# Gathered rows in eight buffers, and two slot computations moved ahead of one transpose: one change to a two-layer MoE kernel

## The chip, the cores and the metric

The kernel runs on 1 core of one Trainium2 chip. The metric is device microseconds of one execution; 163.64 us is the median of 3 runs (163.5 to 164.37). Lower is better. In this text PE is TensorE (PEld its weight loads), DVE is VectorE, ACT is ScalarE, POOL is GpSimd and SP is SyncE.

## The reference

Input is 1,024 tokens of 128 features. Two layers follow each other, each a conditioning step and a mixture of 8 experts, with a residual add:

```python
x = x + L0_ffn(L0_cond(x))     # layer one: every token goes to its 2 best of 8 experts (relu, 512 wide)
x = x + L1_ffn(L1_cond(x))     # layer two: every expert picks its best tokens

# L1_ffn, the part that the second edit touches
n = b * l; k = n * 2 // 8                       # 1024 tokens, 256 for each expert
S = sigmoid(xt @ Wg).T
G, I = top_k(S, k)                              # the 256 best tokens of each expert
ex = xt[I]                                      # gathered rows
hid = gelu(einsum('ekh,ehf->ekf', ex, W1) + b1)
out = (einsum('ekf,efh->ekh', hid, W2) + b2) * G[..., None]
new_x = zeros_like(xt).at[I.reshape(-1)].add(out.reshape(-1, h))
```

## The kernel before, in words

Each engine has one instruction stream, written out by hand, in program order; engines wait for each other on semaphores. Loads and stores go out on SP's queue (some on ACT's); everything indexed goes out on POOL's queue as an indirect DMA, one instruction for 128 rows.

**Layer one.** The 2,048 (token, expert) pairs are sorted by expert into 16 blocks of 128 rows. POOL gathers blocks 1 to 15 into the ring `xs` (`gather(b)`, L454), `RING` buffers deep: gather `b` waits until PE has transposed block `b - RING` out of the same buffer. PE transposes a block (`turn_x(b)`, L592), ACT copies it out of PSUM, and PE does the two matrix products of a block with an expert (`up`, L617; `down0`, L627), 23 such pairs in all, DVE adding the results up (`keep`, L1233). Behind the gathers on POOL stand the 16 scatters of the results (`scatter(b)`, L459); scatter `b` waits for pair `b + 8` to be kept.

**Layer two.** Experts 0 to 6 are computed on gathered rows, 256 each, as units `HEAD` to `UNITS - 1` (`HEAD` is 4: units 0 to 3 are expert 7 done on all tokens). For each of these experts `e` the steps are:

- `place(e)` (DVE, L1369): a one-hot matrix of the rows' places, 128x1024 bf16, double buffered, so `place(e)` waits for `find_slots(e - 2)`.
- `find_slots(e)` (PE, L770): 8 small matmuls with it give the row numbers. For `e` of 2 and more it waits for `index(e - 1)`.
- `index(e)` (DVE, L1116): copies the row numbers to SBUF as integers.
- `gather1(e)` (POOL, L476): two indirect DMAs of 128 rows. Below, gather (e, h) is half h of expert e. All 14 stand in order on POOL's queue; behind them stand the scatters `add(e)` (L483) of the results of experts 0 to 4 into scratch planes in HBM, 10 in all, each waiting for its result in `y1`.
- `turn_xg(e)` (PE, L781): two transposes of the gathered rows; `take_xg(e)` (ACT, L1023) copies them out.
- `up1(n, h)` (PE, L709): four matmuls, `gelu(n, h)` (ACT, L1032), and `down_both(n)` (PE, L818): 16 matmuls.
- `score` (DVE, L1398) writes the result `y1`.

DVE's order is `place(0)`, `place(1)`, `index(0)`, then `index(e - 1)`, `place(e)` in turn for e from 2 to 6, then `index(6)`, then the scores, with the whole-width add `take_dense` (L1427) behind the scores of expert 0. In the end SP loads each plane back in two halves once its scatters have landed, and DVE adds them to the sum (`take_part`, L1416); the results of experts 5 and 6 are spread by PE (L829) instead. ACT's order at the start of the gathered units is `take_xg(0)`, `gelu(4, 0)`, `take_xg(1)`, `gelu(4, 1)`, `gelu(5, 0)`, `take_xg(2)`.

Of the kernel before, what the change touches and what calls it, by code (L numbers as in the profile page):

```python
# [32 lines left out]
H = 256  # L33
K = 2
LORA_SCALE = 32.0 / R
RING = 4
WB_RING = 4
NB = K * T // P
NPAIR = NB + E - 1
# [3 lines left out]
SPARSE = 7  # L43
# [69 lines left out]
def adaln_moe(nc, xT, x, first, second, rows, w1, w2, cond_w, gate_w, v1, c1, v2, consts, out):  # L113
    with ExitStack() as ctx:
        def sb(name, shape, dt=F32):
            return ctx.enter_context(nc.sbuf_tensor(name, shape, dt))

        def sem(name):
            return ctx.enter_context(nc.semaphore(name))
# [90 lines left out]

        xs = sb("xs", [P, RING, C])
        w1_now = sb("w1_now", [P, WB_RING, FW])
# [96 lines left out]

        gathered = [sem(f"gathered_{q}") for q in range(RING)]  # L310
        h0_ready = sem("h0_ready")
# [126 lines left out]
        def _(pool):  # L438
# [7 lines left out]
            def rows_at(idx, i):  # L446
                return bass.IndirectOffsetOnAxis(ap=idx[:, i:i + 1].bitcast(U32), axis=0)
# [3 lines left out]
            def gather(b):  # L451
                if b >= RING:
                    pool.wait_ge(x_turned, b - RING + 1)
                pool.indirect_dma_start(out=xs[:, b % RING], out_offset=None, in_=rows0,  # L454
                                        in_offset=rows_at(gidx, b)).then_inc(gathered[b % RING], 16)

# [45 lines left out]
        def _(pe):  # L502
# [196 lines left out]
            def up1(n, h, parts=(0, 1)):  # L699
                dense, e, q = unit[n]  # L700
                rows_in = dT[:, CAP * q:CAP * q + CAP] if dense else xgT[:, e % 2]
                if not dense:
                    pe.wait_ge(xgT_ready, e + 1)
                u = 2 * n + h
                if u >= 4:
                    pe.wait_ge(h1T_ready, 2 * (u - 4) + 2)
                for f in parts:
                    fc = 2 * h + f
                    mm = pe.matmul(bank[UP_BANKS[u % 4]][:, CAP * f:CAP * f + CAP], v1_sb[:, e, P * fc:P * fc + P],  # L709
                                   rows_in, start=True, stop=True)  # L710
                    if f == 1:
                        mm.then_inc(h1_ready, 1)
# [49 lines left out]
            def find_slots(e):  # L762
                pe.wait_ge(onehot1, e + 1)
                if e < 2:
                    for hlfv_part in hlfv_ready:
                        pe.wait_ge(hlfv_part, e + 1)
                if e >= 2:
                    pe.wait_ge(idx1_ready, 1 if e == 2 else e)
                for c in range(NC):
                    mm = pe.matmul(bank[SLOT_BANKS[e]][:, 0:2 * NH], one1[:, e % 2, :, c],  # L770
                                   hlfv[:, c, e].rearrange("p v h -> p (v h)"), start=(c == 0), stop=(c == NC - 1))
                mm.then_inc(slots1, 1)

            def turn_xg(e):
                pe.wait_ge(gathered1[e], 16 * NH)
                if e == 0:
                    pe.wait_ge(idx1_ready, 2)
                if e >= 1:
                    pe.wait_ge(xgT_ready, e)
                for h in range(NH):  # L780
                    mm = pe.transpose(bank[0][:, P * h:P * h + P], xg[:, e * NH + h, 0:C], ident)  # L781
                mm.then_inc(xg_turned, 1)
# [21 lines left out]
            def down_both(n):  # L804
                e = unit[n][1]
                pe.wait_ge(h1T_ready, 4 * n + 2)
                if n == HEAD:
                    pe.wait_ge(yd_kept, HEAD)
                if n == HEAD + 1:
                    pe.wait_ge(idx1_ready, SPARSE)  # L810
                for g in range(2):
                    if g == 1:
                        pe.wait_ge(h1T_ready, 4 * n + 4)
                    for h in range(NH):
                        if g == 0 and NH * (n - HEAD) + h >= 3:
                            pe.wait_ge(y1_kept, NH * (n - HEAD) + h - 2)
                        for f in (2 * g, 2 * g + 1):
                            mm = pe.matmul(bank[y_bank(n, h)][:, C * h:C * h + C], h1T[:, n % 2, f, P * h:P * h + P],  # L818
                                           v2_sb[:, e, f], start=(f == 0), stop=(f == NF - 1))
                        if g == 1:  # L820
                            mm.then_inc(y1_sent, 1)
# [46 lines left out]
            turn_xg(0)  # L868
            find_slots(3)
            up1(HEAD, 0)  # L870
            turn_xg(1)
            find_slots(4)
            up1(HEAD, 1)
            for n in range(HEAD + 1, UNITS):
                e = n - HEAD
                if 1 < e and e + 1 < SPARSE:
                    turn_xg(e + 1)
                up1(n, 0)
                if n == HEAD + 1:
                    find_slots(SPARSE - 2)  # L880
                    turn_xg(2)
                if n == UNITS - 1:
                    up1(n, 1)
                down_both(n - 1)
                if n == HEAD + 1:
                    find_slots(SPARSE - 1)
                if n < UNITS - 1:
                    up1(n, 1)
# [5 lines left out]
        def _(act):  # L894
# [140 lines left out]
            def take_yd(n):  # L1035
                _, e, q = unit[n]
                act.wait_ge(y1_sent, NH * n + NH)
                act.activation(yd[:, e - SPARSE, NH * q:NH * q + NH], bank[6 + n % 2][:, 0:NH * C], ACT.Copy).then_inc(yd_kept, 1)
# [473 lines left out]
```

## Time and profile before

| | |
|---|---|
| median of 3 runs | 163.64 us (163.5 to 164.37) |
| span of the profiled execution, first to last instruction | 150.0 us |
| profiled execution's own time | the page gives its span alone; the median lies 13.64 us above the span |
| PE busy | 138.6 us, 92% |
| PE weight loads busy | 122.1 us, 81% |
| DVE busy | 94.5 us, 63% |
| ACT busy | 84.9 us, 57% |
| POOL busy | 61.4 us, 41% |
| granted TensorE clock, mean | 0.991 of full speed |

The busy times are averages over stages with different limits. What matters for a change is which wait ends last at the place that it touches; for that the trace is read instruction by instruction, as start, length, engine, line, and what ended the idle time before it. The chain of the page gives 68% of the span to PE, 14% to DVE, 5% to DMA and 3% to POOL.

### The profile page before, as it was taken

The numbers are of one execution on the slowest core, as the hardware profiler recorded it, in microseconds if no ns is written. First come the engines' busy times: TensorE is split into PE (matmuls) and PEld (weight loads), VectorE is DVE, ScalarE is ACT, GpSimd is POOL, SyncE is SP. The second block draws the span as 40 slices with busy tenths as digits, with TensorE's granted clock in tenths as the row PEclk, the third lists the DMA queues.
The fourth block names the chain that finished last, engine by engine and source line by source line (L and its number), as shares of the span: only waits on it lengthen the run. The fifth ranks groups of instructions, "written<-read, shape, count | busy, mean of one in ns | idle before, by whom it ended". The sixth has DMA issues, their size and how long they took to land.

```text
span 150.0 us, 3681 instructions
## 1 busy us (share of the span) xinstructions
PE 138.6 (92%) x1139; PEld 122.1 (81%) x1139; DVE 94.5 (63%) x323; ACT 84.9 (57%) x259; POOL 61.4 (41%) x65
## 2 busy tenths in 40 slices
PE   7999887999999999999999997979998999999970
PEld 3765777999999999964789975748988999999960
DVE  5467947555556565452699777767242597748891
ACT  0688826777777666620377769985326255557400
POOL 5000376544477555560500000003677778777000
PEclk9999999999999999999999999999999999999996
DMA  4999614999999991113602940030022222457714
GB/s 142 357 403 315 216 37 89 312 367 393 394 396 342 300 331 37 38 36 88 211 0 116 400 190 0 0 153 2 19 56 50 56 50 59 152 174 236 254 47 140
DMA packets 12965, 26.10 MB, mean 174 GB/s; under 512 B 2082, under 2 KB 5538, under 8 KB 12562
## 3 DMA queue, kind: packets, MB, share of 16 engines
q1 hardware_dynamic: 10336, 21.54, 40.9%
q0 software_dynamic: 1760, 3.67, 8.1%
q10 hardware_dynamic: 850, 0.66, 1.3%
q8 instruction: 10, 0.16, 0.4%
q14 instruction: 9, 0.07, 0.2%
HBM read 19.92 MB, written 5.93 MB: 172 GB/s over the span
## 4 chain that ended last, share of the span: by engine, by line
PE 68%; DVE 14%; DMA 5%; issue 4%; ACT 3%; POOL 3%; DVEq 0%; ACTq 0%
PE bank L617 13%; PE bank L627 13%; PE bank L709 10%; PE bank L818 7%; PE bank L676 3%; PE bank L581 3%; DVE c_tok L1416 2%; POOL xg L476 2%; PE bank L685 2%; DMA got<-picked 2%; PE bank L508 2%; PE bank L770 2%; DMA xg<-rows,idx 2%; DMA picked<-y,sidx 1%; PE bank L543 1%
## 5 line engine op out<-in xcount | busy, mean ns | idle before, releaser
L952 ACT ACTIVATE hT<-bank,w_now 128x128 f32<-128x128 f32 x88 | 25.1, 368 | 11.5 <-PE bank L617 11.5
L1032 ACT ACTIVATE h1T<-bank,c_sb 128x256 f32<-128x256 f32 x44 | 18.3, 471 | 13.7 <-PE bank L709 13.7
L454 POOL DMA_INDIRECT xs<-rows,gidx x15 | 15.1, 1006 | 24.1 <-DVE gidx L1186 14.6
L627 PE MATMUL bank<-w_sb,hT 128*128 (+1 forms) x184 | 24.4, 276 | 0.3 <-ACT hT L952 0.3
L617 PE MATMUL bank<-xg,w_now 128*128 (+1 forms) x176 | 23.4, 276 | 0.8 <-ACT xg L936 0.8
L627 PEld LDWEIGHTS bank<-w_sb,hT 128*128 128x128 f32 x184 | 22.4, 192 | 0.5 <-ACT hT L952 0.5
L617 PEld LDWEIGHTS bank<-xg,w_now 128*128 128x128 f32 x176 | 21.4, 192 | 1.1 <-issue 1.0
L459 POOL DMA_INDIRECT picked<-y,sidx x16 | 15.7, 979 | 10.0 <-DVE y L1233 8.5
L476 POOL DMA_INDIRECT xg<-rows,idx x14 | 14.8, 1054 | 5.0 <-issue 3.7
L1233 DVE SCALAR_TENSOR_TENSOR y<-bank,pairm,y 128x128 f32 (+1 forms) x23 | 8.1, 351 | 10.2 <-PE bank L627 10.0
L709 PE MATMUL bank<-xgT,v_sb 128*128 128x256 f32 x56 | 14.2, 384 | 0.0
L488 POOL TENSOR_TENSOR hlfv<-hlf1h,cst 128x16 bf16<-128x16 bf16 (+1 forms) x2 | 1.3, 692 | 30.6 <-DVE hlf1h L1365 30.6
L1225 DVE SCALAR_TENSOR_TENSOR y<-b_sb,pairm,y (+1 forms) x23 | 8.1, 351 | 8.5 <-issue 7.8
L818 PEld LDWEIGHTS bank<-v_sb,h1T 128*128 128x128 f32 x96 | 11.6, 192 | 0.3
L483 POOL DMA_INDIRECT plane<-x_sb,idx x10 | 10.5, 1049 | 3.0 <-issue 2.1
L818 PE MATMUL bank<-v_sb,h1T 128*128 128x128 f32 x96 | 11.7, 275 | 0.0
L508 PE MATMUL bank<-ones 128*128 128x512 bf16 x41 | 10.6, 416 | 1.1 <-DVE ones L1118 1.1
L1207 DVE COPY w_now<-w_sb 128x516 f32 (+1 forms) x22 | 9.8, 446 | 2.1 <-issue 1.9
L709 PEld LDWEIGHTS bank<-xgT,v_sb 128*128 128x128 f32 x56 | 9.8, 192 | 1.0
L800 PE MATMUL bank<-v_sb,h1T 128*128 128x128 f32 x80 | 10.1, 278 | 0.0
L800 PEld LDWEIGHTS bank<-v_sb,h1T 128*128 128x128 f32 x80 | 9.5, 192 | 0.2
L709 PE MATMUL bank<-w_eff,v_sb 128*128 128x256 f32 x32 | 9.1, 393 | 0.0
(214 smaller groups left out, 246.9 us busy)
## 6 DMA issues: line engine op xcount, KB each, us to landing
v_sb<-in_v SPq DMA_DIRECT2D x16, 256.0 KB
cw_sb<-in_cond_w SPq DMA_DIRECT2D x8, 386.5 KB
plane<-y SPq DMA_DIRECT2D x5, 512.0 KB, 5.1
w_sb<-plane SPq DMA_DIRECT2D x10, 256.0 KB, 3.1
w_sb<-in_w SPq DMA_DIRECT2D x2, 1024.0 KB, 7.6
w_sb<-in_w SPq DMA_DIRECT2D x1, 1290.0 KB, 7.9
w_sb<-in_w SPq DMA_DIRECT2D x1, 774.0 KB, 5.8
rows<-row SPq DMA_DIRECT2D x1, 544.0 KB, 3.3
```

Of the source, the lines that this page charges most:

```text
L454: pool.indirect_dma_start(out=xs[:, b % RING], out_offset=None, in_=rows0, in_offset=rows_at(gidx, b)).then_inc(gathered[b % RING], 16)
L459: pool.indirect_dma_start(out=picked, out_offset=rows_at(sidx, b), in_=y0[:, b], in_offset=None).then_inc(scattered, 16)
L476: pool.indirect_dma_start(out=xg[:, i], out_offset=None, in_=rows1, in_offset=rows_at(idx1, i)).then_inc(gathered1[e], 16)
L483: pool.indirect_dma_start(out=plane[e], out_offset=rows_at(idx1, i), in_=y1[:, e % Y1_RING, h], in_offset=None).then_inc(added[e], 16)
L508: pe.matmul(out_bank[:], ones[:], ones[:].unsqueeze(1).to_broadcast([P, 4, P]), start=True, stop=True)
L617: mm = pe.matmul(bank[2 + j % 2][:, P * f:P * f + P], w1_of[:, P * f:P * f + P], xsT[:, bass.ds((j - e) * P, P)], start=True, stop=True)
L627: mm = pe.matmul(bank[6 + j % 2][:, 0:C], hT[:, j % 2, P * f:P * f + P], w2_sb[:, bass.ds(e * (NF * C) + f * C, C)], start=(f == 0), stop= ...
L709: mm = pe.matmul(bank[UP_BANKS[u % 4]][:, CAP * f:CAP * f + CAP], v1_sb[:, e, P * fc:P * fc + P], rows_in, start=True, stop=True)
L800: mm = pe.matmul(bank[y_bank(n, h)][:, C * h:C * h + C], h1T[:, n % 2, f, P * h:P * h + P], v2_sb[:, e, f], start=(f == 0), stop=(f == NF ...
L818: mm = pe.matmul(bank[y_bank(n, h)][:, C * h:C * h + C], h1T[:, n % 2, f, P * h:P * h + P], v2_sb[:, e, f], start=(f == 0), stop=(f == NF ...
L952: ins = act.activation(hT[:, j % 2, P * f:P * f + P], bank[2 + j % 2][:, P * f:P * f + P], ACT.Relu, bias=w1_of[:, F + f:F + f + 1])
L1032: act.activation(h1T[:, n % 2, fc], bank[UP_BANKS[(2 * n + h) % 4]][:, CAP * f:CAP * f + CAP], ACT.Gelu, bias=c1_sb[:, e * NF + fc:e * NF ...
```

## The change

The ring of gathered rows of layer one gets eight buffers in place of four. In layer two, PE's stream at the start of the gathered units is put in another order: `turn_xg(1)` comes behind `find_slots(4)` and the second half of the first unit's up-product, and `find_slots(5)` (written `SPARSE - 2`) comes ahead of the second unit's up-product.

```diff
-RING = 4
+RING = 8
@@ -868,16 +868,16 @@
             turn_xg(0)
             find_slots(3)
             up1(HEAD, 0)
-            turn_xg(1)
             find_slots(4)
             up1(HEAD, 1)
+            turn_xg(1)
+            find_slots(SPARSE - 2)
             for n in range(HEAD + 1, UNITS):
                 e = n - HEAD
                 if 1 < e and e + 1 < SPARSE:
                     turn_xg(e + 1)
                 up1(n, 0)
                 if n == HEAD + 1:
-                    find_slots(SPARSE - 2)
                     turn_xg(2)
```

On PE, from the transpose of expert 0's rows to the first down-product of the gathered experts, the rows stood like this (L781 is `turn_xg`, L770 `find_slots`, L709 `up1`, L818 `down_both`):

```order
L781 MATMUL bank<-ident_sb,xg 128x128 x2
L770 MATMUL bank<-hlfv,slot1h 128x4 x8
L709 MATMUL bank<-xgT,v_sb 128x256 x2
L781 MATMUL bank<-ident_sb,xg 128x128 x2
L770 MATMUL bank<-hlfv,slot1h 128x4 x8
L709 MATMUL bank<-xgT,v_sb 128x256 x4
L770 MATMUL bank<-hlfv,slot1h 128x4 x8
L781 MATMUL bank<-ident_sb,xg 128x128 x2
L818 MATMUL bank<-v_sb,h1T 128x128 x8
```

Now they stand like this:

```order
L781 MATMUL bank<-ident_sb,xg 128x128 x2
L770 MATMUL bank<-hlfv,slot1h 128x4 x8
L709 MATMUL bank<-xgT,v_sb 128x256 x2
L770 MATMUL bank<-hlfv,slot1h 128x4 x8
L709 MATMUL bank<-xgT,v_sb 128x256 x2
L781 MATMUL bank<-ident_sb,xg 128x128 x2
L770 MATMUL bank<-hlfv,slot1h 128x4 x8
L709 MATMUL bank<-xgT,v_sb 128x256 x2
L781 MATMUL bank<-ident_sb,xg 128x128 x2
L818 MATMUL bank<-v_sb,h1T 128x128 x8
```

The second L781, expert 1's transpose, moved behind one L770 and one L709; the third L770 moved ahead of the last L709. (The order counts a float32 product as one row; the trace shows it as two matmuls.) The streams of DVE, ACT, POOL and SP keep their order.

On POOL, layer one's gathers and the first scatter, with the semaphores that they wait for, before:

```order
L454 DMA xs<-rows,gidx 128x128 [waits rows0_written,idx_ready]
L454 DMA xs<-rows,gidx 128x128 x2
L454 DMA xs<-rows,gidx 128x128 [waits x_turned] x12
L459 DMA picked<-y,sidx 2048x128 [waits y_kept,sidx_ready]
```

And now:

```order
L454 DMA xs<-rows,gidx 128x128 [waits rows0_written,idx_ready]
L454 DMA xs<-rows,gidx 128x128 x6
L454 DMA xs<-rows,gidx 128x128 [waits x_turned] x8
L459 DMA picked<-y,sidx 2048x128 [waits y_kept,sidx_ready]
```

Four of the fifteen gathers lost their wait for a transpose, and the other eight wait for one that lies four blocks further back.

## Rows read from the trace of the kernel before

**Rows 1.** Page, head of the profile.

```profile
span 150.0 us, 3681 instructions
```

**Rows 2.** Timeline, PE: start us, length us, line, operation, [idle before <- releaser].

```profile
111.40 1.13 PE L709 MATMUL bank<-xgT,v_sb 128*128 128x256 f32 x4
112.99 0.44 PE L781 MATMUL bank<-ident_sb,xg 128*128 128x128 f32 x2 [0.46 <-DMA xg<-rows,idx]
113.27 0.60 PE L770 MATMUL bank<-hlfv,slot1h 128*128 128x4 bf16 x8
113.73 1.97 PE L709 MATMUL bank<-xgT,v_sb 128*128 128x256 f32 x8
115.54 0.60 PE L770 MATMUL bank<-hlfv,slot1h 128*128 128x4 bf16 x8
116.00 0.42 PE L781 MATMUL bank<-ident_sb,xg 128*128 128x128 f32 x2
```

**Rows 3.** Timeline, POOL, gathers of layer two: (1,1), (2,0), (2,1), (3,0), (5,1).

```profile
110.41 0.94 POOL L476 DMA_INDIRECT xg<-rows,idx  x1 [0.30 <-issue]
111.66 1.33 POOL L476 DMA_INDIRECT xg<-rows,idx  x1 [0.30 <-DVE idx L1116]
113.29 0.94 POOL L476 DMA_INDIRECT xg<-rows,idx  x1 [0.30 <-issue]
114.53 0.95 POOL L476 DMA_INDIRECT xg<-rows,idx  x1 [0.30 <-issue]
...
120.79 1.51 POOL L476 DMA_INDIRECT xg<-rows,idx  x1 [0.30 <-issue]
```

**Rows 4.** Timeline, DVE, same stretch: places 4, 5, 6, index 4, the dense add.

```profile
111.49 0.68 DVE L1369 TENSOR_TENSOR slot1h<-xT_sb,loc 128x1024 bf16<-128x1024 bf16 x1
113.91 0.16 DVE L1116 TENSOR_REDUCE idx<-bank 128x2 int32<-128x4 f32 x1 [1.74 <-PE bank L770]
113.99 0.68 DVE L1369 TENSOR_TENSOR slot1h<-xT_sb,loc 128x1024 bf16<-128x1024 bf16 x1
...
116.26 0.68 DVE L1369 TENSOR_TENSOR slot1h<-xT_sb,loc 128x1024 bf16<-128x1024 bf16 x1
...
120.27 1.22 DVE L1427 TENSOR_TENSOR w_sb<-w_sb,c2b_sb 128x1024 f32<-128x1024 f32 x1
```

**Rows 5.** Timeline, ACT, gelu(4, 0) and take_xg(1).

```profile
112.63 0.84 ACT L1032 ACTIVATE h1T<-bank,c_sb 128x256 f32<-128x256 f32 x2 [1.28 <-PE bank L709]
113.47 0.38 ACT L1023 ACTIVATE xgT<-bank 128x256 f32<-128x256 f32 x1
```

**Rows 6.** Timeline: POOL's first and last add, DVE's scores of expert 4.

```profile
125.16 1.05 POOL L483 DMA_INDIRECT plane<-x_sb,idx  x1 [0.30 <-issue]
...
137.42 0.96 POOL L483 DMA_INDIRECT plane<-x_sb,idx  x1 [0.30 <-issue]
133.38 0.80 DVE L1398 SCALAR_TENSOR_TENSOR x_sb<-bank,xg,gb 128x128 f32<-128x128 f32 x2 [2.38 <-PE bank L818]
```

**Rows 7.** Timeline and DMA issues, the tail: last plane load, DVE's last six adds.

```profile
140.03 0.43 SPq L378 DMA_DIRECT2D w_sb<-plane  x1
w_sb<-plane SPq DMA_DIRECT2D x1, 256.0 KB, 4.9
141.66 3.98 DVE L1416 TENSOR_TENSOR c_tok<-c_tok,w_sb 128x512 f32<-128x512 f32 x6
```

**Rows 8.** Layer one: landing of its gathers (min/median/max), timeline of PE and POOL.

```profile
DMA to landing us min/median/max: 2.4/5.6/6.8
34.79 0.27 PE L592 MATMUL bank<-ident_sb,xs 128*128 128x128 f32 x1
27.75 0.94 POOL L454 DMA_INDIRECT xs<-rows,gidx  x1 [0.66 <-PE bank L592]
41.11 0.94 POOL L454 DMA_INDIRECT xs<-rows,gidx  x1 [0.95 <-PE bank L592]
49.05 0.97 POOL L459 DMA_INDIRECT picked<-y,sidx  x1 [0.45 <-DVE y L1233]
```

## The prediction

> **What bounds the kernel now.** I read the page first, then the waits, then the timelines of the two stretches that the diff touches, then the tail. The span is 150.0 us and the median of the runs 163.64 us, so 13.64 us lie around the span [rows 1]; I make the sum in span time and carry that difference over unchanged, since nothing of it is touched.
>
> In layer one PE runs back to back. In layer two there is one hole in front of it, at `turn_xg(1)`: the transpose starts at 112.99 after 0.46 us in which PE waited for gather (1,1) to land [rows 2]. The part that the busy shares hide is POOL: it is 41% busy, but from gather (1,1) at 110.41 [rows 3] to the end of the last add at 138.38 [rows 6] it never waits for anybody. Each gather takes 0.94 us and the next follows 0.30 us later, so 1.25 us apart [rows 3], and the adds go on at once from 125.16 to 137.42 [rows 6]. The last add (4,1) could have started at 134.18, when its score was written, 3.2 us before it did [rows 6]. So the adds hang on POOL's own pace, not on PE.
>
> In the tail the two paths meet. The last plane half is issued at 140.03 and lands 4.9 us later, at 144.93; DVE's six adds run from 141.66 to 145.64, one each 0.66 us, so the sixth, which needs that half, starts near 144.96 [rows 7]. PE's path (over the last scores and DVE) and POOL's path (over adds and loads) reach the end within 0.1 us of each other. **A gain on PE alone is therefore worth nothing at the end, and a loss on either is paid in full.**
>
> **Eight buffers in layer one: 0.** Gather 8 started at 27.75, when a transpose had freed its buffer, and its block was transposed at 34.79, 7.04 us later; the gathers landed 5.6 us (median) and at worst 6.8 us after their start [rows 8]. That is 0.24 us of margin in the worst case, and no transpose waited. With eight buffers POOL goes at 1.25 us a gather: the last starts near 27.75 + 7 x 1.25 = 36.5 in place of 41.11, 4.6 us earlier [rows 3, 8]. The first scatters can follow earlier, but by scatter 5 (49.05) they wait for DVE's sums, as before [rows 8]. What could be hidden here has been hidden already; what hides it is PE's work, and if that cover were gone the wait would be at most 0.24 us per block from the worst landing alone. Cost: the gathers share the DMA engines with the weight loads earlier, with unchanged bytes. A bound from below and above is the spread of landing itself, 5.6 against 6.8 us, 1.2 us on a load; no PE instruction of this stage waits for a load, so I take 0.
>
> **The new order in layer two, on PE.** `up1(4, 0)` starts at 111.40; eight such matmuls take 1.81 us (113.73 to 115.54), so four 0.90: PE is free at 112.30 [rows 2]. `find_slots(4)` no longer stands behind the transpose. Its one-hot is ready (place 4 ends at 112.17 [rows 4]), so it starts at 112.30 in place of 113.27, 0.97 us earlier; it takes 0.46 us to the next product [rows 2]. The moved steps issue no DMA; POOL asks for the row numbers of expert 4 only at 114.53 + 2 x 1.25 = 117.03 [rows 3], and had them since 114.07 [rows 4], so having them earlier starts no gather earlier. `up1(4, 1)` goes to 113.66, and `turn_xg(1)` then finds its rows landed since 112.99: the wait of 0.46 us is gone. `find_slots(5)` follows 0.28 us later, at 113.94 (its one-hot: below). `up1(5, 0)` needs ACT's copy of the transpose. Before, that copy began 0.48 us behind the transpose and took 0.38 [rows 2, 5]; with some 0.05 for the signal PE can go on at 113.66 + 0.91 = 114.57, 0.17 us after `find_slots(5)`. Its four matmuls end at 115.47, and PE stands before `turn_xg(2)`, 0.53 us earlier than its start at 116.00 before [rows 2].
>
> **What it waits for there.** Gather (1,1) ended at 111.35 on POOL and its rows were used at 112.99, 1.64 us later. Gather (2,1) ends at 114.23 [rows 3], so its rows are there at 115.87 and no earlier. Of the 0.53 us won only 0.13 are left, if POOL stays as it was. The stall is not removed, it is moved to the next expert.
>
> **What moves on POOL.** It does not stay as it was. Gather (2,0) started at 111.66 inside place 4 (111.49 to 112.17) and took 1.33 us in place of 0.94; gather (5,1) at 120.79 inside the dense add (120.27 to 121.49) took 1.51 [rows 3, 4]. Both were longer by what was left of the DVE operation less some 0.12 us (0.51 left, 0.39 longer; 0.70 left, 0.57 longer). Gather (2,1), which ran when place 5 began at 113.99, took 0.94, and (3,0), 0.14 us before its end, 0.95. So a gather that starts in such an operation stands until it is over.
>
> The Trainium skill ("SBUF — State Buffer", section "Who interferes with whom") says that a DVE instruction with two SBUF inputs holds off a GpSimd one that reads SBUF for its whole length, and the first comer wins; the trace agrees for these two. The same section infers that this kind, tensor_tensor, leaves descriptor generation alone; by that the two hits below would not come, and the sum would be 163.5. The rows decide.
>
> With `find_slots(4)` at 112.30, index 4 comes 0.64 us later as before (113.27 to 113.91), at 112.94, and place 5 runs from 113.02 to 113.70 [rows 2, 4]. Gather (2,1) starts at 113.29, inside it: 0.41 left, 0.29 longer. `find_slots(5)` at 113.94 gives index 5 at 114.58 and place 6 from 114.66 to 115.34; gather (3,0), now at 114.82, is inside that one: 0.52 left, 0.40 longer. Before, place 6 ran at 116.26 and held up nobody.
>
> So the rows of (2,1) are there at 115.87 + 0.29 = 116.16, and `turn_xg(2)` starts 0.16 us **later** than before. From there PE has no other wait, so all of it, and DVE's scores behind it, is 0.16 us late. POOL is late by 0.69 us, until the dense add: it runs at 120.43 to 121.65, gather (5,1) starts at 121.48 inside it, 0.17 left, 0.05 longer in place of 0.57. POOL is then 0.69 - 0.52 = 0.17 us late. This is a catch: whoever starts in the dense add ends with it, so POOL's delay becomes DVE's own. Both paths reach the tail 0.16 to 0.17 us late. **Sum:** 150.0 + 0.17 + 13.64 = 163.81 us, 0.1% more.
>
> **The rivals.**
> - *No new hits* (the DVE places miss the gathers' starts by some tenths, or do not hold them off). `turn_xg(2)` at 115.87, 0.13 us earlier; the dense add 0.13 earlier, which holds (5,1) to the same end: 163.64 - 0.13 = 163.51. For: place 5 is hit with 0.27 us to spare on one side, but the second hit hangs on the first (without it gather (3,0) starts at 114.53, ahead of place 6). 27%.
> - *PE's gain arrives whole*: the 0.46 us of waiting [rows 2] go and the tail follows, 163.18. Against it: the last half lands when DVE needs it, and gather (2,1) paces. 8%.
> - *Slower, by POOL*: a delay on POOL that the dense add does not catch. It decides once POOL is late by more than 0.86 us (121.65 - 120.79), one more hit of 0.3 or so; then every tenth is paid at the end over the adds and plane loads, and an add is hit as gathers are. With one more hit of 0.57, the longest seen: 0.69 + 0.57 - 0.86 = 0.40 beyond what is caught, on top of 0.16: 164.2. Two more hits: 164.8. 12%, half of it over the bound below.
> - *Eight buffers do nothing that a time shows*: this is part of the forecast, not against it.
>
> **How the numbers follow.** Forecast 163.8 with 48%, no new hits 163.5 with 27%, whole gain 163.2 with 8%, slower by POOL 164.2 and up with 12%; 5% for what I don't see. About 0.5% (0.82 us) is what a measurement of this kernel can tell from no change. Of the cases only the last half of the POOL one (6%) and a share of the unseen lie above 164.46, and only unseen ones and a lucky tail below 162.82. The range, from the whole gain to the first steps of the POOL case: 163.2 to 164.4, which also takes the spread of the runs.
>
> **What the profile of the changed kernel would show.** Right: no PE wait at `turn_xg(1)`, one of 0.5 to 0.7 us at `turn_xg(2)`, for the gather's DMA; gather (2,1) and (3,0) longer than 1.1 us, (5,1) near 1.0; POOL without a wait from first gather to last add; in layer one the fifteenth gather near 36.5. Wrong: `turn_xg(2)` below 115.9; gathers of 0.94 throughout; a wait of PE for a weight load; a last plane half that lands over 0.3 us from DVE's need, which would let one path win alone.

## The result, and the profile after

The changed kernel takes 168.46 us (median of 4 runs, 167.37 to 172.47) and the kernel before 164.0 us (4 runs, 163.5 to 168.1). The ratio is 1.034, 95% interval 1.026 to 1.041: about 3% slower. The forecast was 163.8 with a range up to 164.4, so it is wrong. Ratios here and below leave disturbed runs out, so they can differ from the quotient of the medians of all runs; where they do so noticeably, both are given.

The first thing to read is the head of the page, since the profiled run is one of those 4 and has a time of its own: 167.37 us.

```profile
span 165.6 us, 3681 instructions
PE 144.6 (87%) x1139; PEld 126.6 (76%) x1139; DVE 93.8 (57%) x323; ACT 85.4 (52%) x259; POOL 61.3 (37%) x65
...
PEclk9999999957999999999999999999999699999999
```

Only 167.37 - 165.6 = 1.8 us lie around the span. The forecast had taken 13.64 us for that, the distance from the median to the span before [rows 1]. The profile before therefore shows an execution of about 150.0 + 1.8 = 151.8 us, some 12 us shorter than any of the times that stood beside it. So those 12 us must lie inside the span of the executions that were timed, and no row of the profile before shows them.

The trace after shows where such time goes. This is its timeline around the first such stretch, PE first, then ACT, DVE and POOL (start, length, engine, line, operation, and in brackets the idle time before and what ended it; "remote" is a releaser that the profile could not name, and no other core runs here):

```profile
25.76 0.27 PE L592 MATMUL bank<-ident_sb,xs 128*128 128x128 f32 x1
26.39 1.15 PE L617 MATMUL bank<-xg,w_now 128*128 x8 [0.36 <-issue]
27.38 1.06 PE L627 MATMUL bank<-w_sb,hT 128*128 x8
28.28 0.27 PE L592 MATMUL bank<-ident_sb,xs 128*128 128x128 f32 x1
33.60 2.07 PE L617 MATMUL bank<-xg,w_now 128*128 x8 [5.05 <-issue]
35.46 1.91 PE L627 MATMUL bank<-w_sb,hT 128*128 x8
37.17 0.42 PE L592 MATMUL bank<-ident_sb,xs 128*128 128x128 f32 x1
37.38 1.91 PE L617 MATMUL bank<-xg,w_now 128*128 x8
39.09 1.08 PE L627 MATMUL bank<-w_sb,hT 128*128 x7
...
32.92 0.37 ACT L936 ACTIVATE xg<-bank,first_sb 128x128 f32<-128x128 f32 x1 [5.80 <-remote]
32.96 0.35 DVE L1233 SCALAR_TENSOR_TENSOR y<-bank,pairm,y 128x128 f32<-128x128 f32 x1 [7.21 <-remote]
33.15 0.94 POOL L454 DMA_INDIRECT xs<-rows,gidx  x1 [2.15 <-remote]
```

PE's last product of a pair ends at 27.38 + 1.06 = 28.44, and its transpose at 28.55. DVE, which adds that product up, starts at 32.96, 4.5 us behind it; ACT, which copies the transpose, at 32.92, 4.4 us behind; POOL, which waits for a transpose too, at 33.15. Three engines with different jobs begin within 0.23 us, and what they have in common is that each waits for PE, whose work had been done for over 4 us. (The profile models where a matmul ends, but PE works in order, and the transpose behind that product starts at 28.28.) The whole core does not stand still: POOL starts two gathers that have nothing left to wait for, at 28.80 and 30.05, and between 28.6 and 32.9 the DMA engines are 97% busy. PE waits for ACT's copy and is idle for 5.05 us. Behind that, eight matmuls take 1.91 to 2.07 us where the same took 1.06 to 1.15 before the pause. The windows show the clock of that stretch (busy time of PE, its loads, DVE, ACT and POOL, granted clock, DMA share, GB/s):

```profile
0.00:25.00 25.00, 22.04 (x144) 15.79 (x145) 16.28 (x56) 14.10 (x29) 7.79 (x11) 1.00 0.65 226
25.00:40.00 15.00, 9.59 (x59) 9.13 (x58) 3.63 (x11) 5.24 (x19) 7.74 (x8) 0.77 0.82 277
```

The granted clock is 0.77 on average there: behind the idle stretch PE ran at the lower of its two levels (1.2 GHz, by the doubled lengths) until some 39 us, then at 2.4 GHz again. The next such pause is in layer two, the same view of PE, DVE and ACT:

```profile
120.57 1.13 PE L709 MATMUL bank<-xgT,v_sb 128*128 128x256 f32 x4 [0.52 <-issue]
121.72 0.66 PE L770 MATMUL bank<-hlfv,slot1h 128*128 128x4 bf16 x8
122.24 1.11 PE L709 MATMUL bank<-xgT,v_sb 128*128 128x256 f32 x4
123.19 0.38 PE L781 MATMUL bank<-ident_sb,xg 128*128 128x128 f32 x2
127.42 0.66 PE L770 MATMUL bank<-hlfv,slot1h 128*128 128x4 bf16 x8 [3.85 <-DVE slot1h L1369]
...
126.60 0.16 DVE L1116 TENSOR_REDUCE idx<-bank 128x2 int32<-128x4 f32 x1 [4.93 <-remote]
123.80 0.84 ACT L1032 ACTIVATE h1T<-bank,c_sb 128x256 f32<-128x256 f32 x2 [3.28 <-PE bank L709]
126.70 0.38 ACT L1023 ACTIVATE xgT<-bank 128x256 f32<-128x256 f32 x1 [2.06 <-remote]
```

`find_slots` was done at 122.38 and DVE reads it at 126.60, 4.2 us later; the transpose was done at 123.57 and ACT reads it 3.1 us later, and again both begin together. In between one signal did come, late too: the first unit's product was done at 121.70, and ACT's gelu of it starts at 123.80. The DMA engines are 21% busy from 121 to 127. The names of what PE waits for ("issue", "DVE slot1h") are those of the work that it needed next. That work was waiting for PE's own signals.

So the slower time is not made of what the diff's steps cost. In the text below a pause is such a stretch: PE's work done, and its signals with the other engines late, by 2.1 to 4.6 us here and by up to 7.2 us in a trace below.

### The profile page after: what moved, and what is told of

It reads as the page before. It is cut to its first block, busy times and chain, and to the rows that moved or that the text cites. A ratio compares the mean times of both kernels' runs of the same rounds, so it can differ in the third digit from the quotient of the medians.

```text
span 165.6 us, 3681 instructions
## 1 busy us (share of the span) xinstructions
PE 144.6 (87%) x1139; PEld 126.6 (76%) x1139; DVE 93.8 (57%) x323; ACT 85.4 (52%) x259; POOL 61.3 (37%) x65
## 4 chain that ended last, share of the span: by engine, by line
PE 64%; DVE 12%; issue 8%; ACT 6%; DMA 4%; another core or an unknown queue 3%; ACTq 1%; POOL 0%; DVEq 0%
PE bank L617 13%; PE bank L627 13%; PE bank L709 10%; PE bank L818 6%; PE bank L800 3%; PE bank L770 2%; DMA got<-picked 2%; PE bank L676 2%; PE bank L685 2%; DVE c_tok L1416 2%; PE bank L508 2%; PE bank L518 2%; DMA picked<-y,sidx 1%; PE bank L543 1%
## 5 line engine op out<-in xcount | busy, mean ns | idle before, releaser
L617 PE MATMUL bank<-xg,w_now 128*128 (+1 forms) x176 | 25.3, 290 | 6.2 <-issue 5.4
L617 PEld LDWEIGHTS bank<-xg,w_now 128*128 128x128 f32 x176 | 23.1, 204 | 6.9 <-issue 6.9
L1032 ACT ACTIVATE h1T<-bank,c_sb 128x256 f32<-128x256 f32 x44 | 18.3, 472 | 18.2 <-PE bank L709 17.0
L627 PE MATMUL bank<-w_sb,hT 128*128 (+1 forms) x184 | 25.5, 283 | 0.3 <-ACT hT L952 0.3
L627 PEld LDWEIGHTS bank<-w_sb,hT 128*128 128x128 f32 x184 | 23.5, 200 | 0.5 <-ACT hT L952 0.5
L459 POOL DMA_INDIRECT picked<-y,sidx x16 | 15.5, 971 | 17.8 <-DVE y L1233 17.4
L709 PE MATMUL bank<-xgT,v_sb 128*128 128x256 f32 x56 | 15.2, 402 | 0.5 <-issue 0.5
L818 PEld LDWEIGHTS bank<-v_sb,h1T 128*128 128x128 f32 x96 | 12.5, 203 | 1.3 <-ACT h1T L1032 1.0
L818 PE MATMUL bank<-v_sb,h1T 128*128 128x128 f32 x96 | 12.7, 286 | 0.8 <-ACT h1T L1032 0.8
L483 POOL DMA_INDIRECT plane<-x_sb,idx x10 | 9.9, 992 | 5.1 <-DVE x_sb L1398 2.7
L936 ACT ACTIVATE xg<-bank,first_sb 128x128 f32<-128x128 f32 x16 | 6.0, 377 | 10.5 <-remote 5.8
L709 PEld LDWEIGHTS bank<-xgT,v_sb 128*128 128x128 f32 x56 | 10.2, 198 | 1.6 <-issue 0.6
L800 PE MATMUL bank<-v_sb,h1T 128*128 128x128 f32 x80 | 10.1, 278 | 0.0
L1116 DVE TENSOR_REDUCE idx<-bank 128x2 int32<-128x4 f32 x7 | 1.1, 162 | 15.6 <-PE bank L770 10.6
```

Of the source, the lines that this page charges most:

```text
L459: pool.indirect_dma_start(out=picked, out_offset=rows_at(sidx, b), in_=y0[:, b], in_offset=None).then_inc(scattered, 16)
L483: pool.indirect_dma_start(out=plane[e], out_offset=rows_at(idx1, i), in_=y1[:, e % Y1_RING, h], in_offset=None).then_inc(added[e], 16)
L617: mm = pe.matmul(bank[2 + j % 2][:, P * f:P * f + P], w1_of[:, P * f:P * f + P], xsT[:, bass.ds((j - e) * P, P)], start=True, stop=True)
L627: mm = pe.matmul(bank[6 + j % 2][:, 0:C], hT[:, j % 2, P * f:P * f + P], w2_sb[:, bass.ds(e * (NF * C) + f * C, C)], start=(f == 0), stop= ...
L1032: act.activation(h1T[:, n % 2, fc], bank[UP_BANKS[(2 * n + h) % 4]][:, CAP * f:CAP * f + CAP], ACT.Gelu, bias=c1_sb[:, e * NF + fc:e * NF ...
```

## The experiments

Two facts sort everything else. Beside the other kernels, the kernel before took 152.7 to 152.9 us (median) on three chips and 163.5 to 164.0 us in four groups of runs on others, one chip twice. No chip on record gave both. And none of the ten executions traced on the first sort (nor the profile before) has a pause, while all nine traced on the second have one in each layer. I call them quiet and pausing chips. None of those nine is of the kernel before itself; the nearest are one with an added fill on POOL and one with the new order alone. Nor is a quiet chip wholly quiet: 19 of 209 executions there, of the kernel before and of the edits alike, took 157.9 to 159.8 us, and none of those was traced. The forecast's steps, with costs of tenths of a microsecond, can only be tested on a quiet chip; the measured loss only on a pausing one.

**The kernel before, unchanged, and the parts one by one** (a quiet chip, where the kernel before takes 152.76 us, 35 runs).

> The kernel before, unchanged. Theory A (whole-core pauses: the changed kernel's trace has two stretches near 26 to 33 us and 121 to 127 us in which the other engines get nothing from TensorE for about 5 us each, and these, not the moved instructions, are the loss): the kernel before has such pauses too in most executions, since its time of 163.64 us lies 13.64 us above the span of its profile, while the changed kernel's lies 1.8 us above; so this run's profile shows a span near its time less 1.8 us, mostly near 162, with one or two pauses of about 5 us. Theory B (only the changed kernel pauses): span 150.0 again and a time 13.6 us above it.

> Only the eight buffers of layer one, the order of layer two as before. Theory R (the gathers that run ahead bring on the pause in layer one): ratio 1.02 to 1.035 to the kernel before. Theory O (the new order in layer two brings on the second pause): ratio 1.00, within 0.5%.

```diff
-RING = 4
+RING = 8
```

> Only the new order in layer two, four buffers. Theory O: ratio 1.02 to 1.035. Theory R: 1.00. If the two edits each cost half, both come out near 1.015.

```diff
             up1(HEAD, 0)
-            turn_xg(1)
             find_slots(4)
             up1(HEAD, 1)
+            turn_xg(1)
+            find_slots(SPARSE - 2)
...
                 if n == HEAD + 1:
-                    find_slots(SPARSE - 2)
                     turn_xg(2)
```

> The changed kernel unchanged. Under either theory the ratio of the first measurement, 1.0335, within 1.02 to 1.045. If it comes out near 1.00 the first measurement was of pauses that come and go with chip or moment.

| kernel | median us | ratio to before, 95% |
|---|---|---|
| before again | 152.41 | 0.997 (0.992 to 1.001) |
| eight buffers alone | 152.90 | 1.001 (0.997 to 1.005) |
| order alone | 152.74 | 1.000 (0.997 to 1.004) |
| the whole change | 153.25 | 1.002 (0.997 to 1.006) |

None of the four can be told from no change, and the whole change least of all from the forecast's 1.001. The trace of the whole change there (span 151.0 us) shows the forecast's steps. Timeline of PE, DVE (places 5 and 6) and POOL (gathers (2,1), (3,0), (5,1)):

```profile
112.14 1.13 PE L709 MATMUL bank<-xgT,v_sb 128*128 128x256 f32 x4
113.10 0.61 PE L770 MATMUL bank<-hlfv,slot1h 128*128 128x4 bf16 x8
113.57 1.11 PE L709 MATMUL bank<-xgT,v_sb 128*128 128x256 f32 x4
114.52 0.38 PE L781 MATMUL bank<-ident_sb,xg 128*128 128x128 f32 x2
114.73 0.60 PE L770 MATMUL bank<-hlfv,slot1h 128*128 128x4 bf16 x8
115.37 1.13 PE L709 MATMUL bank<-xgT,v_sb 128*128 128x256 f32 x4
117.02 0.44 PE L781 MATMUL bank<-ident_sb,xg 128*128 128x128 f32 x2 [0.52 <-DMA xg<-rows,idx]
...
113.83 0.68 DVE L1369 TENSOR_TENSOR slot1h<-xT_sb,loc 128x1024 bf16<-128x1024 bf16 x1
115.45 0.68 DVE L1369 TENSOR_TENSOR slot1h<-xT_sb,loc 128x1024 bf16<-128x1024 bf16 x1
...
114.02 1.30 POOL L476 DMA_INDIRECT xg<-rows,idx  x1 [0.30 <-issue]
115.63 1.32 POOL L476 DMA_INDIRECT xg<-rows,idx  x1 [0.30 <-DVE idx L1116]
...
122.25 1.08 POOL L476 DMA_INDIRECT xg<-rows,idx  x1 [0.30 <-issue]
```

The wait at `turn_xg(1)` is gone and one of 0.52 us stands at `turn_xg(2)`. Gather (2,1), which starts 0.19 us into place 5, takes 1.30 us, and (3,0), 0.18 us into place 6, takes 1.32. What is left of place 5 less what gather (2,1) got longer is 0.49 - 0.36 = 0.13 us, of place 6 0.50 - 0.38 = 0.12, where the forecast had taken 0.12. The repeated kernel before has the wait at `turn_xg(1)`:

```profile
111.54 1.13 PE L709 MATMUL bank<-xgT,v_sb 128*128 128x256 f32 x4
113.29 0.44 PE L781 MATMUL bank<-ident_sb,xg 128*128 128x128 f32 x2 [0.62 <-DMA xg<-rows,idx]
...
116.66 0.44 PE L781 MATMUL bank<-ident_sb,xg 128*128 128x128 f32 x2 [0.23 <-DMA xg<-rows,idx]
```

From the start of the first up-product to `turn_xg(2)` it takes 5.12 us; the change takes 4.88, and the profile before took 4.60 [rows 2], with no wait at the second transpose. So this distance differs by half a microsecond between two executions of the same kernel, three times the forecast's 0.16. The moved stall is real, and the ratios say that it is small. Its sign shows faintly over all quiet traces: from the start of gather (1,0), which lies ahead of the edit, to the end, seven traces with the old order take 40.8 to 41.9 us (mean 41.4) and four with the new one 41.1 to 42.2 (mean 41.7).

**The same on another quiet chip, and the change with its gathers paced** (before 152.70, 35 runs).

> Only the eight buffers. Two chips have shown two pictures: on one the kernel before takes 152.8 us and every variant the same; on the other it takes 163.5 us, TensorE hangs twice for several us in each execution, and the changed kernel is 2.0% longer, its first hang 5.0 us and early in layer one (28.6 us from the start) where kernels with three or four buffers have one of 2.4 to 3.5 us later (near 46 to 51 us). Theory R (the gathers that run ahead bring that hang forward and lengthen it): where the kernel before takes over 160 us this one is at 1.015 to 1.03. Theory O (the order does it): 1.00.

> Only the new order of layer two. Theory R: 1.00 to 1.005 on either chip. Theory O: 1.015 to 1.03 where the kernel before takes over 160 us.

> The kernel before, unchanged, for a trace of the same chip. Both theories: ratio 1.00; where it takes over 160 us, its trace has a hang of 2.4 to 3.5 us near 48 us and one with DVE waiting 4.9 us for the row numbers of expert 4.

They gave 152.78 us, 0.999 (0.996 to 1.003); 153.01 us, 1.001 (0.997 to 1.005); and 152.40 us, 0.999 (0.995 to 1.003). The fourth kernel has the change's eight buffers and its order, but a gather waits for the transpose four blocks back, as with four buffers:

> The changed kernel with its eight buffers, but each gather of layer one still waits for the transpose four blocks back, so that nothing runs ahead. Theory R in its narrow form (running ahead is what matters): like the order alone, 1.00 to 1.005. If the buffers' place in SBUF or their semaphores matter: like the changed kernel, 1.02 to 1.03 where the kernel before takes over 160 us.

```diff
             def gather(b):
-                if b >= RING:
-                    pool.wait_ge(x_turned, b - RING + 1)
+                if b >= 4:
+                    pool.wait_ge(x_turned, b - 4 + 1)
```

153.04 us, 1.002 (0.999 to 1.005). On a quiet chip the pacing is worth nothing either way, and the question that this kernel was made for, what pacing does to the measured loss, stays undecided for the whole change.

**On a pausing chip: the change again, and three other edits** (before 163.53 us, 17 runs).

> The changed kernel once more, at another time. Theory P (pauses of the whole core, of about 5 us each, come with the moment and chip and not with the edits): the ratio is near 1.00 wherever the kernel before takes 152 to 153 us; where the kernel before takes over 160 us, both have pauses, and the ratio scatters around 1.00 by a pause more or less, 0.97 to 1.04. Theory Q (the edits bring on more pauses where there are any): there the ratio is 1.02 to 1.04 again.

> The kernel before with one more operation on POOL's stream, a clearing of an 128x1024 tile that nobody reads any more, between the last gather and the first add; with the step to the next instruction about 1.25 us. Forecast's theory (POOL's path over adds and plane loads meets PE's path at the end within 0.1 us): 1.1 to 1.3 us longer, ratio 1.008. Rival (only PE's path sets the end): ratio 1.000.

```diff
             pool.wait_ge(zeroed, 16 * PLANES)
+            pool.memset(zero, 0.0)
```

> The kernel before with three buffers for layer one's rows. Forecast's theory (four buffers cover the landing with a margin of some tenths, so eight are worth nothing): with three a block's transpose can come no earlier than 0.3 + 0.3 + 5.6 = 6.2 us after the one three blocks back, 2.05 us a block where PE needs 1.90, so transposes wait for gathers and the kernel is 1 to 2.5 us longer, ratio 1.006 to 1.016. Rival (landings shorten as fewer rows are under way): no wait, ratio 1.00.

> Only expert 1's transpose is moved, behind slots 4 and the first unit's second up-product; slots 5 stay behind the second unit's up-product. By the theory that a gather that starts inside a whole-width DVE operation lasts until it ends: gather (2,1) 1.2 to 1.35 us as in the changed kernel, gather (3,0) 0.95 us where the changed kernel has 1.3, since place 6 starts some 1.5 us later. If the lengthening came from the transposes or from PE's order itself, (3,0) is long here too.

```diff
             up1(HEAD, 0)
-            turn_xg(1)
             find_slots(4)
             up1(HEAD, 1)
+            turn_xg(1)
```

The change took 166.91 us, 1.020 (1.013 to 1.027): the loss comes back, smaller than the 1.034 before. Its trace has the pause of the trace after, PE idle for 5.05 us at `up` (L617) with ACT released after 5.81 us. The traces of the late POOL and of the half-way order, both with four buffers, have it later (DVE at 54.72 and 54.62) and shorter, 2.7 us. These three traces are late from the start: their first gather starts at 23.6 us, where it starts at 17.4 to 18.5 in all others. In the trace of the change PE's sixteen matmuls at 8.72 take 3.42 us, where those at 7.01 in the trace after take 1.85. So their pauses stand some 5.7 us later than they otherwise would: those at 54.7 near 49. The late POOL took 163.15 us, 1.007 (0.998 to 1.017), by the medians 0.998. Its added fill of 0.97 us stands in the trace, and 1.007 is what the forecast's rule for POOL (paid at the end) expects, but the interval holds 1 and the medians say otherwise, so it shows only that a microsecond on POOL doesn't cost 3%. It does not test the rule: in this trace POOL waits 1.54 us for a score behind the fill, at 147.92, where the forecast had counted on a POOL that never waits. Three buffers took 167.29 us, 1.016 (1.005 to 1.027), by the medians 1.023, as slow as eight. Transposes wait for gathers there (0.56 and 0.22 us at two of those between 25 and 45 us), as the expectation had it, but its pause is longer too (PE idle for 3.51 us at 54.23, then at the lower clock for 6.7 us, by a granted clock of 0.79 over 52 to 68 us), so the ratio does not confirm the reason. The half-way order was run once, 168.44 us, with the late start of the late POOL's profiled run (167.7), so its time tells nothing; what gather (3,0) does in it could not be read, since a pause lies on that place.

**Which part, on a pausing chip** (before 163.71 us, 11 runs).

> Only the eight buffers. Theory R: 1.015 to 1.03 where the kernel before takes over 160 us, 1.00 where it takes 153. Theory O: 1.00 on both.

> Only the new order. Theory O: 1.015 to 1.03 where the kernel before takes over 160 us. Theory R: 1.00 to 1.005 on both.

Eight buffers alone: 167.37 us (165.0 to 172.03), 1.015 (1.000 to 1.031), by the medians 1.022. The order alone: 164.81 us (163.85 to 165.52), 1.014 (1.005 to 1.023), by the medians 1.007. Both are above before, the first only just, and the times do not rank them. The traces tell them apart: with eight buffers alone the first pause is in layer one's gathers, at 25 to 34 us, as after; with the order alone DVE has its first pause before 49.03 (2.73 us), the place where all kernels with four buffers, or paced as four, have it (released at 48 to 49 us, or at 54.6 to 54.7 in the two traces with the late start).

**Is it the buffers or the run-ahead?** First on a chip that turned out quiet (before 152.86):

> Eight buffers, each gather of layer one still waiting for the transpose four blocks back; order as before. If running ahead brings the hang forward: like the kernel before, 0.995 to 1.005, first hang near 47 us with DVE without a signal for 2.3 to 2.7 us. If size, place or semaphores do: 1.015 to 1.025 where the kernel before takes over 160 us, first hang at 26 to 33 us with 7.2 us. Where it takes 153 us both give 1.00.

> Eight buffers free to run ahead, beside the paced ones: 1.015 to 1.025 again where the kernel before takes over 160 us, the hang of 7.2 us at 26 to 33 us.

152.84 us, 1.001 (0.997 to 1.004), and 152.38 us, 0.996 (0.992 to 1.000): nothing, as on every quiet chip. Then the same two kernels on a pausing chip (before 163.88 us, 16 runs), the test that decides:

> Eight buffers paced as four. If running ahead matters: 0.995 to 1.005 on any chip, and where the kernel before takes over 160 us the first hang near 47 us. If size, place or semaphores matter: 1.015 to 1.025 there, hang at 26 to 33 us.

> Eight buffers free: 1.015 to 1.025 where the kernel before takes over 160 us, else 1.00.

| eight buffers, order as before | median us | ratio to before, 95% |
|---|---|---|
| paced as four | 164.28 (161.2 to 165.54) | 0.992 (0.986 to 0.999) |
| not paced | 166.34 (164.56 to 167.42) | 1.015 (1.009 to 1.021) |

By the medians of all runs the paced one stands at 1.002 and the other at 1.015, so the size of the gap is 1.3 to 2.3%, but it is there by either count. The two kernels have the same buffers and differ only in which transpose POOL's gathers wait for. Windows of the paced kernel's trace (span 161.0 us), columns as above:

```profile
25.00:40.00 15.00, 14.54 (x130) 14.31 (x130) 8.19 (x24) 11.63 (x41) 7.87 (x9) 1.00 0.93 329
42.00:55.00 13.00, 10.22 (x78) 10.04 (x78) 4.67 (x14) 6.23 (x23) 6.57 (x7) 0.87 0.72 250
```

And of the kernel that isn't paced (span 163.8 us):

```profile
25.00:40.00 15.00, 10.27 (x72) 9.48 (x72) 4.49 (x13) 6.34 (x23) 8.31 (x9) 0.89 0.78 249
42.00:55.00 13.00, 13.00 (x118) 12.97 (x117) 6.92 (x20) 9.52 (x35) 4.38 (x5) 1.00 0.88 283
```

The pause has changed its place, from the second window to the first. In the paced kernel PE is idle for 0.46 + 2.78 = 3.24 us of the two windows, in the other for 4.73; each has one window at a lower clock, 0.87 and 0.89. The timelines at those places, DVE and PE of the paced kernel, and its third gather of layer two, (1,0):

```profile
48.13 0.35 DVE L1233 SCALAR_TENSOR_TENSOR y<-bank,pairm,y 128x128 f32 x1 [2.78 <-remote]
48.89 2.07 PE L627 MATMUL bank<-w_sb,hT 128*128 x8 [2.78 <-ACT hT L952]
...
114.04 0.94 POOL L476 DMA_INDIRECT xg<-rows,idx  x1 [0.30 <-issue]
```

PE, ACT and DVE of the other. It has its full speed back only at 33.51, after a further wait, and a third follows at 37.34. DVE's product was done at 24.60 + 1.06 = 25.66 and is read at 32.88, 7.2 us later, while ACT got one signal at 27.68: not all of them come at once.

```profile
24.60 1.06 PE L627 MATMUL bank<-w_sb,hT 128*128 128x128 f32 x8
...
27.68 0.37 ACT L936 ACTIVATE xg<-bank,first_sb 128x128 f32<-128x128 f32 x1 [4.02 <-remote]
28.36 1.90 PE L617 MATMUL bank<-xg,w_now 128*128 x8 [2.59 <-issue]
...
33.51 1.15 PE L617 MATMUL bank<-xg,w_now 128*128 x8 [1.36 <-issue]
...
37.34 1.15 PE L627 MATMUL bank<-w_sb,hT 128*128 x8 [0.78 <-issue]
...
32.88 0.35 DVE L1233 SCALAR_TENSOR_TENSOR y<-bank,pairm,y 128x128 f32<-128x128 f32 x1 [7.38 <-PE bank L627]
```

The start of layer one's first gather and that of gather (1,0), which lies ahead of the edited part of layer two, split a span in three. For traces of both sorts, in us:

| kernel | first gather | gather (1,0) | between the two | from (1,0) to the end |
|---|---|---|---|---|
| quiet: before again; eight buffers; order; both | 18.1; 18.3; 17.8; 18.5 | 109.3; 109.8; 109.3; 109.9 | 91.2; 91.5; 91.5; 91.4 | 41.8; 41.4; 41.8; 41.1 |
| pausing, four buffers: late POOL; half-way order | 23.6; 23.6 | 119.3; 119.2 | 95.7; 95.6 | 46.6; 47.4 |
| pausing, four buffers: order alone | 18.3 | 114.9 | 96.7 | 47.8 |
| pausing: eight buffers paced | 17.4 | 114.0 | 96.6 | 47.0 |
| pausing: eight buffers, two groups of runs | 17.9; 17.7 | 116.3; 116.1 | 98.4; 98.5 | 47.0; 47.7 |
| pausing: the change, the profile after and again | 17.9; 23.6 | 117.9; 123.2 | 100.0; 99.6 | 47.7; 47.1 |
| pausing: three buffers | 17.6 | 118.3 | 100.7 | 46.9 |

(The last column is the span less the mark. The spans are 151.1, 151.2, 151.1, 151.0; 165.9, 166.6; 162.7; 161.0; 163.3, 163.8; 165.6, 170.3; 165.2.) Behind the mark all pausing traces lie between 46.6 and 47.8 us, 5 to 7 us above the quiet ones, whatever the edit. Between the two gathers all eleven quiet traces, the profile before among them, take 91.2 to 91.7 us, and the pausing ones sort by how far the gathers run ahead: 95.6 to 96.7 with four buffers or paced as four, 98.4 and 98.5 with eight. So eight buffers add 1.9 us over the paced kernel, all of it ahead of the mark. The order alone is level with the paced kernel there (96.7 and 96.6).

The whole change adds another 1.2 to 1.6 us in that stretch to what eight buffers alone take, although up to the mark both kernels run the same instructions. The clock goes with it: after the first pause both traces of the change have the lower level for 6.8 to 6.9 us (granted clock 0.77 over 25 to 40 us; 0.83 over 30 to 50 in the late one), both traces of eight buffers alone for 3.3 us (0.89 over 25 to 40 us). Why, with the same instructions, is not known, and two traces of each can't say whether it is the rule.

## Why the prediction was wrong, point by point

**What bounds the kernel: the failed step.** "So 13.64 us lie around the span ... I make the sum in span time and carry that difference over unchanged, since nothing of it is touched." 1.8 us lie around the span, in every profiled run that has a time of its own (167.37 - 165.6, 152.92 - 151.1, 162.83 - 161.0). The other 12 us lie inside the span. In the kernels traced on pausing chips they are pauses in layers one and two and what follows from them; the trace in hand was free of them. That the difference was too large to be an overhead could have been seen as an open question. I took it for a constant, and with it took for granted that executions with and without pauses answer to an edit alike. The Trainium skill ("Runtime: NRT & Kernel Launch", section "The ~15µs preamble/postamble breakdown") gives a gap of some 6.2 us by which the profile's total is longer than the reported execution time, whatever the kernel. No run here shows that total. Here the reported time is the longer one, by 1.8 us over the span, so that gap could not have stood for the 13.64 us.

**Eight buffers: 0.** As a sum of waits this was right: in the quiet trace below the last gather starts at 36.70 us (36.5 forecast), and the scatters wait for DVE's sums from the first on, at 40.85, not only by scatter 5. The timeline of POOL with eight buffers alone:

```profile
36.70 0.94 POOL L454 DMA_INDIRECT xs<-rows,gidx  x1 [0.30 <-issue]
40.85 0.99 POOL L459 DMA_INDIRECT picked<-y,sidx  x1 [3.21 <-DVE y L1233]
```

The measured ratios on three quiet chips are 1.001, 0.999 and 0.996. On pausing chips the ratio is 1.015, 2.5 us, and the range had no room for it. What was mis-sized is this term: 0 against 1.9 us (traces) to 2.5 us (ratio) there. That the gathers' run-ahead makes it, and not the buffers, is shown by the paced kernel, which has the buffers and not the cost, in one pair of kernels on one chip; the place of the first pause and the time between the two gathers sort the other traces in the same way. Why a run-ahead of POOL brings a pause of PE's signals forward, and makes it longer, is not shown.

**The new order.** The mechanism was right in each step on quiet chips: no wait at `turn_xg(1)`, 0.52 us at `turn_xg(2)`, gathers (2,1) and (3,0) at 1.30 to 1.31 and 1.32 us in all four quiet traces with the new order (forecast 1.23 and 1.34), (5,1) at 0.94 to 1.09 (forecast near 1.0), no wait on POOL up to the last add. The rival without new hits is refuted by both gathers. The place in the Trainium skill ("SBUF — State Buffer", "Who interferes with whom") that infers that tensor_tensor leaves descriptor generation alone is contradicted twice more, by 0.36 and 0.38 us. The cost, 0.17 us or 0.1%, fits the four quiet ratios of the order (1.000 and 1.001) and of both parts (1.002, and 1.002 with the gathers paced), and is below what they can tell. On a pausing chip the order alone came out at 1.014 (medians: 1.007), measured once. Its trace is as long as that of the paced kernel between the two gathers and 0.8 us longer behind the mark, one trace each. Over all pausing traces the new order takes 47.1 to 47.8 us behind the mark and the old one 46.6 to 47.7, so no cost of the order is shown there. And its moved steps do not make the loss: what the change takes more than the kernels with four buffers, 3.0 to 4.4 us, stands ahead of the mark, where those steps have not yet run.

**The rivals.** Slower by POOL had 12%, and it had the side right, as the forecast itself had, but both by luck: the trace after shows neither POOL's delay nor the forecast's 0.17 us as the loss. A delay of about 1 us on POOL was made, and the upper end of its interval is 1.7%, on a pausing chip, where POOL has waits that hide such a delay. *PE's gain arrives whole* is refuted on quiet chips by the wait of 0.52 us at `turn_xg(2)`. The outcome belongs to none of the cases. It was in the 5% for what I don't see, and with that the range was too narrow by the error of the base, not by that of a term.

**What stays open.** Why PE's signals arrive late at all, on some chips and not on others, with the same instructions, was not found; nor can the profile tell a late signal from a result that is late behind it. Traffic alone is not it: the DMA engines are 97% busy in the first pause after and 21% in the second. Nor, in that trace, is it a late fetch of instructions: its DMA view has no packet of the two instruction queues from 28 to 34 us, nor from 121 to 127.5. A pause comes in layer two in every trace of a pausing chip, whatever the edit. The loss was 3.4 and 2.0%, and twice 1.5% with eight buffers alone; what sets the size is not known, nor whether chip or moment makes a chip pausing. A paced kernel also has other instructions on POOL, and an effect of their place in memory was not tested apart. The change with its gathers paced ran on a quiet chip only.

## What to carry to other kernels

Before any sum, compare the profiled execution's time with the runs it stands beside: where the median lies much further above the span than in other profiled runs (1.8 us here), the profile shows another kind of execution than the one that is timed, and what an edit costs in the missing part is unknown, in both directions. Then the range has to be widened by a part of the missing time, here 12 us, however clean the sum of the steps is. And a buffer that only lets a hidden engine run further ahead is not free of risk: keeping the old pace with the new buffers costs one wait and separates the two.

## What the runs showed of the hardware

- Signals of PE can be late, several at once. At 32.92, 32.96 and 33.15 us three engines are released by work that ended 4.4 to 4.6 us before, while POOL goes on with what it need not wait for; in another trace DVE's signal is 7.2 us late and reaches it 5.2 us after one that reached ACT. The medians of the kernel before differ by 11 us of 164 (163.7 against 152.8) between chips whose traces have such pauses and chips whose traces have none; the kernel before itself was not traced with them.
- What such a pause costs can be more than its length: after 5.05 us without work, PE's eight matmuls took 1.91 us in place of 1.06 until some 39 us. After 2.35 and 2.61 us (late POOL, half-way order) the granted clock stayed at 1.00. Between the two gathers those traces take 95.6 to 95.7 us, and the two that had the lower clock for some 3.4 us 96.6 to 96.7.
- The same kernel, the same code, has medians of 152.7 to 152.9 us in some groups of runs and 163.5 to 164.0 in others, 7% apart. Eight buffers are worth nothing on one sort (0.996 to 1.001) and cost 1.5% on the other, the whole change 1.002 and 2.0 to 3.4%.
- A gather on POOL that starts within a whole-width DVE operation on two tiles (0.68 us) takes 1.30 to 1.32 us in place of 0.94, in all four quiet traces with the new order.
